# A transformer block on one core: the second attention's output projection and the two normalisations behind it as one block by chunks

## What is computed

```python
x = x + 0.5 * _L0_ffn_ref(_layernorm(x), ...)      # step 1
x = x + _L0_attn_ref(_layernorm(x), ...)           # step 2
x = x + 0.5 * _L0_ffn_ref(_layernorm(x), ...)      # step 3
x = x + 0.5 * _L1_ffn_ref(_layernorm(x), ...)      # step 4, see below
x = x + _L1_attn_ref(_layernorm(x), ...)           # step 5, see below
x = x + 0.5 * _L1_ffn_ref(_layernorm(x), ...)      # step 6, as step 4

def _layernorm(x, eps=1e-05):
    return (x - mean(x)) / sqrt(var(x) + eps)      # over the 128 columns of a row

# the end of _L1_attn_ref: f is the attention's output, 128 wide
    y = f @ Wo.T + bo
    mu, var = mean(y), mean((y - mu) ** 2)
    return x + ln_w * (y - mu) * rsqrt(var + 1e-05) + ln_b    # x is the normalised input of the step

# _L1_ffn_ref: a router picks 2 of 8 experts from its input
    scores = x @ w_gate
    ...
```

## Time and profile before

| | us |
|---|---|
| median of 3 runs (2874.14 to 2876.14) | 2874.9 |
| the profiled execution | 2879.6 |
| its span, first to last instruction | 2877.9 |
| granted TensorE clock over the span, share of full speed | 0.941 |

### The profile page before, as it was taken

One profiled execution on the slowest core, in us unless ns is written; L12 is line 12 of the kernel. 1 busy time (PEld: TensorE's weight loads), 2 busy tenths in 40 slices (PEclk: granted clock), 3 DMA queues, 4 the chain that ended last, 5 costly groups with the idle time before them and its releaser, 6 DMA issues. The chain is left out here.

```text
span 2877.9 us, 60111 instructions
## 1 busy us (share of the span) xinstructions
PE 2457.7 (85%) x18614; PEld 1009.4 (35%) x18614; DVE 2437.3 (85%) x3916; ACT 2254.0 (78%) x2520; POOL 2005.8 (70%) x1255
## 2 busy tenths in 40 slices
PE   4848999997659986999999999999999999983898
PEld 3833333334655662222222222222222222222566
DVE  6778888884676657999999999999999999986765
ACT  4655777776445546899999999999999999992554
POOL 5541222222634656799999999999999999993455
PEclk9978999998678997999999999999999999996799
DMA  4241000000220002000000000000000000000000
GB/s 144 62 128 32 29 28 28 28 28 7 65 63 1 1 1 101 17 18 14 14 15 16 17 14 14 15 14 17 15 14 14 15 16 16 14 1 1 1 12 19
DMA packets 96687, 76.57 MB, mean 27 GB/s; under 512 B 32592, under 2 KB 78168, under 8 KB 96448
## 3 DMA queue, kind: packets, MB, share of 16 engines
q1 hardware_dynamic: 92288, 66.36, 7.9%
q0 software_dynamic: 4288, 8.82, 0.9%
HBM read 47.77 MB, written 24.42 MB: 25 GB/s over the span
## 5 line engine op out<-in xcount | busy, mean ns | idle before, releaser
L1960 POOL TENSOR_TENSOR a_sg<-a_sg,all_f0w 128x1568 f32<-128x1568 f32 x256 | 904.9, 3535 | 21.4
L2103 ACT ACTIVATE a_pt<-a_pb 128x1024 f32<-128x1024 f32 x512 | 698.1, 1363 | 13.6 <-PE a_pb L2010 13.6
L2178 DVE TENSOR_REDUCE a_mx<-a_pm 128x1 f32<-128x1024 f32 x507 | 613.7, 1210 | 13.5 <-PE a_pm L2010 11.9
L2189 DVE TENSOR_SCALAR a_sg<-a_pa 128x1024 int32<-128x1024 int32 x512 | 615.3, 1202 | 8.0 <-PE a_pa L2010 8.0
L2112 ACT ACTIVATE a_sg<-a_sg,a_parh 128x2048 f32<-128x2048 f32 x256 | 599.7, 2343 | 15.3 <-POOL a_sg L1960 15.3
L2028 PE MATMUL a_po<-a_pt,a_Vh 128*32 128x512 f32 x2048 | 541.1, 607 | 64.7 <-ACT a_osb L2122 62.5
L2116 ACT ACTIVATE a_sg<-a_sg 128x2048 f32<-128x2048 f32 x256 | 578.7, 2261 | 0.1
L2028 PE MATMUL a_po<-a_sg,a_Vh 128*32 128x512 f32 x2048 | 541.1, 607 | 0.0
L1957 POOL TENSOR_SCALAR all_f0w<-a_sg,a_parh 128x1568 f32<-128x1568 f32 x256 | 513.8, 2007 | 31.3 <-DVE a_sg L2189 28.6
L1770 ACT ACTIVATE a_pt<-a_ring 128x1024 f32<-128x1024 f32 (+2 forms) x384 | 313.7, 846 | 150.7 <-PE a_ring L1697 147.3
L1842 DVE TENSOR_REDUCE a_mx<-a_ring 128x2 f32<-128x1024 f32 (+3 forms) x384 | 359.1, 955 | 74.3 <-PE a_ring L1680 55.3
(11 more groups left out here) (282 smaller groups left out, 4578.8 us busy)
## 6 DMA issues: line engine op xcount, KB each, us to landing
all_Q<-q_parts SPq DMA_DIRECT2D x256, 48.0 KB
all_K<-k_parts SPq DMA_DIRECT2D x256, 48.0 KB
k_parts<-p_parts SPq DMA_DIRECT2D x16, 384.0 KB, 3.0
e_recs<-routed_rows SPq DMA_DIRECT2D x70, 64.5 KB, 1.8
all_Q<-a_rows SPq DMA_DIRECT2D x256, 2.0 KB
q_parts<-p_parts SPq DMA_DIRECT2D x16, 192.0 KB, 2.4
q_parts<-p_parts SPq DMA_DIRECT2D x8, 384.0 KB, 2.6
a_Vh<-all_V SPq DMA_DIRECT2D x64, 36.0 KB, 1.8
```

What stands on the lines that cost most here:

```text
L1960: nc.gpsimd.tensor_tensor(buf[:, :, 0:CUT], buf[:, :, 0:CUT], sums, ALU.mult)\
L2103: nc.scalar.activation(pt[(j - LT) % 4][:, i, :], pb[:], ACT.Exp, scale=SC)\
L2178: nc.vector.tensor_reduce(mx[:, (j // PER) % 2, t:t + 1], top[:], AX.X, ALU.max)\
L2189: nc.vector.tensor_scalar(sg[(j - ls) % 4][:, i, :].bitcast(I32), pa[:].bitcast(I32), SIGN_OFF, None, ALU.bitwise_and).then_inc(abs_done, 1)
```

## The change

`ln_transposed` is replaced by `norm_split`, and for the second attention `project_out` is drawn into it (argument `front`); `project_out` itself is left with the first attention's case alone. The new block goes by chunks of 4 tiles in steps: in step s, chunk s is turned, chunk s-1 is projected and its statistics and scale are made, chunk s-2 gets its first normalisation, chunk s-3 is added to X and gets its second statistics and scale, chunk s-4 is normalised, chunk s-5 is turned and leaves PSUM, chunk s-6 goes to the router. Without `front` (n4) the same loop begins at s = 2 and holds the later half alone.

Both normalisations move from DVE to ACT (`normalise_y`, `normalise`: one instruction per tile, scale and bias per row, as `norm_project` does). The Newton step gets another form and a last instruction that makes the bias. POOL adds ln_b for all 8 chunks at the block's start, then does one chunk's multiplication by ln_w and one chunk's low part per step. With `front` the turned rows go to the buffer `all_V` in place of `all_XNT`, which still holds the attention's output; without it the incoming rows of n4 are loaded into `all_XNT`.

```diff
-def ln_transposed(nc, tag, X, XNT, ident, split=None, router=None, incoming=None):
+def norm_split(nc, tag, X, XNT, ident, split, router, incoming=None, front=None):
...
+        steps = range(0 if front else 2, NCH + 6)
...
             @block.vector
...
+                def scale(c, var_ready, root_ready, steps_done, root, t, var, inverse, agg, shift, done):
+                    k = tiles(c)
+                    dve.wait_ge(var_ready, c + 1)
+                    dve.wait_ge(root_ready, c + 1)
+                    link = Chain(dve, steps_done, 3 * c)
+                    link(nc.vector.tensor_tensor(t[:, k], root[:, k], root[:, k], ALU.mult))
+                    link(nc.vector.scalar_tensor_tensor(t[:, k], t[:, k], -0.5, var[:, k], ALU.mult, ALU.mult))
+                    link(nc.vector.scalar_tensor_tensor(inverse[:, k], t[:, k], 1.5, root[:, k], ALU.add, ALU.mult))
+                    nc.vector.scalar_tensor_tensor(shift[:, k], agg[:, k, 0], -1.0, inverse[:, k], ALU.mult, ALU.mult)\
+                        .then_inc(done, 1)
...
+                for s in steps:
+                    if front and inside(s - 1):
+                        attended(s - 1)
+                    if inside(s - 3):
+                        rows(s - 3)
+                    if front and inside(s - 1):
+                        scale(s - 1, yve_ready, yrs_ready, ynewton, yrs, yt, yve, yrstd, ymv, yoffset, yscaled)
+                    if inside(s - 3):
+                        scale(s - 3, ve_ready, rs_ready, newton, rs, t1, ve, rstd, mv, offset, scaled)
...
             @block.gpsimd
...
+                if front:
+                    pool.wait_ge(weights_in, loads)
                     for c in range(NCH):
-                        low(c)
+                        nc.gpsimd.tensor_tensor(X[:, tiles(c), :], X[:, tiles(c), :],
+                                                lb[:].unsqueeze(1).broadcast_to([P, 4, D]), ALU.add).then_inc(lb_added, 1)
+                for s in steps:
+                    if front and inside(s - 2):
+                        weigh(s - 2)
+                    if inside(s - 5):
+                        low(s - 5)
...
             @block.scalar
...
+                def normalise(c):
+                    act.wait_ge(scaled, c + 1)
+                    if c >= XR:
+                        act.wait_ge(turned, c - XR + 1)
+                    for q in range(4):
+                        k = 4 * c + q
+                        nc.scalar.activation(xn[:, c % XR, q, :], X[:, k, :], ACT.Identity, bias=offset[:, k:k + 1],
+                                             scale=rstd[:, k:k + 1]).then_inc(xn_ready, 1)
...
+                for s in steps:
+                    if front and inside(s - 2):
+                        normalise_y(s - 2)
+                    if inside(s - 4):
+                        normalise(s - 4)
+                    if front and inside(s):
+                        copy_in(s)
+                    if front and inside(s - 1):
+                        root(s - 1, yve_ready, yve, yrs, yln_var, yrs_ready)
+                    if inside(s - 3):
+                        root(s - 3, ve_ready, ve, rs, ln_var, rs_ready)
+                    if inside(s - 5):
+                        evacuate(s - 5)
...
             @block.tensor
...
+                for s in steps:
+                    if front and inside(s - 1):
+                        project(s - 1)
+                    if front and inside(s):
+                        turn_in(s)
+                    if inside(s - 5):
+                        turn(s - 5)
+                    if inside(s - 6):
+                        route(s - 6)
...
-            lambda: project_out(nc, "o5", X, tiles, ident, a1, a1_in, True),
-            lambda: ffn_second("6", out_v),
+            lambda: ffn_second("6", out_v, front=(tiles, a1, a1_in)),
```

More of the change, by code:

```diff
@@ L97, in ln_transposed @@
         mv = m.sb("mv", [P, NT, 2])
[L98 to L112, removed]
+        ve, rs, t1, rstd, offset = (m.sb(n, [P, NT]) for n in ("ve", "rs", "t1", "rstd", "offset"))
+        xn = m.sb("xn", [P, XR, 4, D])
+        pt = m.ps("pt", [P, 2, CH])
+        psr = m.ps("psr", score.shape)
@@ L119, in _ @@
                 def _(sp):
[L120 to L123, removed]
+                    for c in range(NCH):
+                        sp.dma_start(XNT[:, c * CH:(c + 1) * CH].rearrange("p (k d) -> p k d", d=D),
+                                     incoming[c * CH:(c + 1) * CH, :].rearrange("(k p) d -> p k d", p=P))\
+                            .then_inc(came[c], 16)
@@ new lines, in _ @@
+                if front:
+                    dve.wait_ge(weights_in, loads)
+                for s in steps:
[7 more added lines that the diff above has]
+                        scale(s - 3, ve_ready, rs_ready, newton, rs, t1, ve, rstd, mv, offset, scaled)
@@ L207, in _, with turn_in, project @@
+                act.wait_ge(routed, 1)
+                nc.scalar.activation(score[:], psr[:], ACT.Copy).then_inc(scored, 1)
             @block.tensor
             def _(pe):
+                def turn_in(c):
+                    if c >= 2:
+                        pe.wait_ge(f_copied, c - 1)
+                    for q in range(4):
+                        last = nc.tensor.transpose(ptr[:, c % 2, q * P:(q + 1) * P], F[4 * c + q], ident[:])
+                    last.then_inc(f_turned, 1)
+                def project(c):
+                    pe.wait_ge(f_copied, c + 1)
+                    if c >= 2:
+                        pe.wait_ge(y_in, c - 1)
+                    for q in range(4):
+                        last = nc.tensor.matmul(psy[:, c % 2, q, :], fT[:, c % 2, q * P:(q + 1) * P], woT[:],
+                                                start=True, stop=True)
+                    last.then_inc(y_done, 1)
@@ L210, in route, with turn @@
+                def turn(c):
+                    pe.wait_ge(xn_ready, 4 * c + 4)
+                    if c >= 2:
+                        pe.wait_ge(evacuated, c - 1)
+                    for q in range(4):
+                        last = nc.tensor.transpose(pt[:, c % 2, q * P:(q + 1) * P], xn[:, c % XR, q, :], ident[:])
+                    last.then_inc(turned, 1)
                 def route(c):
@@ L1379, in _ @@
             def _(act):
-                def copy(c):
+                for c in range(NCH):
                     act.wait_ge(turned, c + 1)
@@ L2280, in ffn_first, with ffn_second @@
                           returned, n, *((begin, loaded) if n == 0 else ()))
-        def ffn_second(tag, out=None, incoming=None):
+        def ffn_second(tag, out=None, incoming=None, front=None):
             with ExitStack() as inner:
```

250 lines of the change are left out of this document (89 added, 161 removed).

## The result

The changed kernel takes 2856.9 us (median; 2855.0 to 2857.4), the kernel before 2875.5 beside it: a ratio of 0.9933, interval 0.9916 to 0.9950, or 18.6 us less. The forecast was 2857.3 us and 17.6 us less. The profiled execution took 2857.0 us, with a span of 2855.3.

What follows compares the result with a forecast made beforehand. The bound was taken to be DVE's queue plus a lead-in and lead-out that other engines do not overlap. Joined block -12.8 us (66.9 for 79.7) and n4 -4.8 sum to -17.6, giving 2857.3 us; range 2848 to 2867.

Steps and rivals of the forecast that it cites:

- DVE's work: Joined block: additions, statistics and Newton steps take DVE 5.5 us a chunk, 44.0 us for 8 chunks.
- Lead-in, roots, lead-out: Joined block: 4.1 us to the first bias addition, 2.6 us of root waits in four steps, 6.7 us at the end.
- Waits behind GpSimd: Joined block: DVE instructions held up by POOL, 9.5 us in sum: 2.7 in chunk 0, 5.6 at multiplications, 1.2 at low parts.
- The last term: Last two steps of the joined block: POOL's low part meets DVE's addition to X, 1.2 us (0 to 9).
- the prediction's first reading of rows 6: Old kernel's trace: a DVE instruction of 0.17 us took 2.31 because POOL's multiplication was running, ending at 2640.02.
- n4: Fourth normalisation by chunks: 3.4 us a chunk, lead-out 6.7, low parts 0.5; 37.3 us against 42.1, -4.8 us.
- ACT and PE: Joined block: a step is 6.0 us of work for ACT, and 6.0 us for PE at half clock.
- (b): ACT and DVE go in lockstep; root waits of 0.8 us in some 9 steps lose 7 us: 2864.5; chance 0.2.
- the cover of the roots: Joined block: ACT's roots are ready 0.5 us before DVE wants them; each further delay costs its own length.
- (a): POOL costs DVE nothing, its instructions find the gaps: 57.4 and 36.8 us, time 2847.3 us; chance 0.2.
- (c): The gain is given back by ACT's load and longer waits: block 78 us, n4 unchanged, time 2873; chance 0.06.
- (d): Slower: POOL and DVE always exclude each other, block 85.4 us, n4 46.0, +9.6 us, time 2884.5; chance 0.04.

Runs made afterwards that it cites:

- the extra one: Whole change plus one more GpSimd multiplication of 512 columns in each of 8 steps: joined stretch 67.4 us against 65.4, 18.0 us less than the kernel before.
- the improved version: Whole change with three edits together (ln_b additions early, no variance instruction, rows of X first): joined stretch 57.4 us, 25.4 us less than the kernel before.
- the last run: Whole change with those three edits, and GpSimd instead of ScalarE makes the high parts: joined stretch 59.1 us, 23.0 us less than the kernel before.
- the two halves: Two runs with one half of the change each: n4 only, 5.4 us less than the kernel before; o5 and n6 joined only, 14.1 us less.

## Why the prediction was right, point by point

**DVE's work.** 5.5 us a step was too much by 0.18. Without waits a step takes 5.32 us (2620.41 to 2625.72 in the run with GpSimd's work made small). The statistics had been priced to the end of the variance instruction; where nothing waits for that one, the next starts 0.08 us after it, not 0.17 (2633.47 and 2633.55 above). That is 1.4 us for 8 chunks, and nearly all of the 1.5 us by which the block is shorter than forecast (65.4 against 66.9); two other errors, of about 1 us each, cancel, as the next two paragraphs show.

**Lead-in, roots, lead-out.** First bias addition at 2600.58, 4.0 us behind the first turn (4.1 forecast); four root waits shown as about 0.6 (0.65); from the last Newton instruction's start to the end of the scores 6.85 us (6.7). The third root wait, in step 9, was priced too low: with GpSimd's work made small it is 1.61 us, because ACT's normalising stands ahead of that root. In the whole change 1.0 of it is hidden under the overlong variance instruction.

**Waits behind GpSimd.** 9.5 us forecast, 9.4 found as overlong instructions, 8.4 of them on the path: chunk 0 about 2.5 (2.7), seven variance instructions of y 5.9 together (5.6), one at the end 1.0 (1.2). They came as 1.2 or as 0.6 us long, by the phase, and not as 1.0 each. The last term was wrong in its mechanism, and its size is luck: the low parts at the end come 0.3 us behind the addition to X, so the addition keeps its 0.69 us and GpSimd waits (1.43 us instead of 1.16). What takes 1.18 us there is X's variance instruction, behind the last multiplication, and that cost nothing. That these are waits behind GpSimd is shown by the runs that move or shrink its work (2.5 and 7.6 us back), and that they cost only where the instructions meet, by the extra one. The multiplication that the prediction's first reading of rows 6 rests on, the one that ends at 2640.02, is not among those rows; before the change it was

```profile
2636.75 3.27 POOL L1407 TENSOR_TENSOR o_y<-o_y,all_lw 128x1024 f32<-128x1024 f32 x1 [2.96 <-DVE o_y L1447]
```

**n4.** 37.3 forecast, 36.3 found: a step takes 3.33 us instead of 3.4 (again the end of the statistics), and the 0.5 us allowed for low parts were not needed. There GpSimd waits: its low parts, which come 0.3 us behind VectorE's additions, show 1.42 us instead of 1.15, the additions 0.69.

```profile
842.25 0.69 DVE L177 TENSOR_TENSOR all_X<-all_X,all_XNT 128x512 f32<-128x512 f32 x1
...
845.58 0.68 DVE L177 TENSOR_TENSOR all_X<-all_X,all_XNT 128x512 f32<-128x512 f32 x1
...
848.90 0.69 DVE L177 TENSOR_TENSOR all_X<-all_X,all_XNT 128x512 f32<-128x512 f32 x1
```
```profile
849.18 1.42 POOL L207 TENSOR_TENSOR 4_XL<-all_XNT,4_XH 128x512 f16<-128x512 f32 x1 [21.11 <-ACT all_XNT L256]
```

**ACT and PE.** 6.0 us a step was too much for both. ACT's row of four takes 1.65 us, but the next row begins about 1.55 after its start, and a copy of 0.58 is followed after 0.48; a full step is 5.35 us (the three windows of the improved version). PE is busy for 5.29 at half clock. Since both lay under VectorE's 5.7 to 6.3 us, this did no harm here; but for rival (b) it made the cover of the roots look thinner than it was, and VectorE waits for no root in a full step.

**The rivals.** (a) is wrong by 8.4 us of waits on the path; its own figure, 2847.3 us, lies just outside the range that is said to hold most of it. (b) did not happen in this kernel's full steps, but the three edits together come near it: 5.41 us a step, ACT full, VectorE waiting for roots 0.35 us a step (0.20 and 0.15); the loop through ACT and VectorE is the next limit, as far as the last run shows it. (c): no loss can be seen, by the two halves. (d) is refuted by the extra instruction.

**The total.** The two stretches gave -20.1 us (-14.3 and -5.8) where -17.6 were summed; the medians differ by 18.6 and the two profiled executions by 22.6. The profiled execution of before lay 4.7 us above the median of the runs shown, that of after 0.1 above its own, so a distance carried over as if it were fixed was not. That the median was met to 0.4 us is therefore better than the sum deserves; what held is the working by stretches, to 1.5 and 1.0 us.

## What to carry to other kernels

Where one engine's instructions hold up another's, as GpSimd's did VectorE's here, price the neighbour by where its instruction falls, not by how long it is: 1.26 us of GpSimd under VectorE's statistics cost nothing, the same 1.26 us against an instruction of 0.17 cost up to 1.1, and taking away the instruction that was hit moved the wait to the next one. Joining two stages paid here when the fullest engine gave up work at the same time (10.0 us for both); with the normalising left on it, the joined form was slower than the two blocks. Price steps from start to start, in rows of the same form, and ask of the last instruction of a price whether the next one really waits for it.

## What the runs showed of the hardware

- VectorE's waits behind GpSimd are hidden in durations: an instruction of 128x4 elements took 0.62 to 1.26 us instead of 0.16, and none of that was shown as idle time.
- An instruction with one input in SBUF waits too: the variance TENSOR_SCALAR (0.17 us) took up to 1.23. BATCH_NORM_STATS2 (0.87 for four), its aggregation (0.36 for four) and an addition with one input in PSUM (0.65 to 0.69) never did, beside any GpSimd instruction. "Who interferes with whom", in "SBUF — State Buffer" of the Trainium skill, counts tensor_scalar among the operations that can use both ports, which agrees; it doesn't name the statistics instructions.
- GpSimd loses as well when it comes second: 1.76 us for a multiplication of 1.27.
- PE's granted clock was 0.50, the lower of its two levels, in all of the joined block but two steps, where it was 0.77 on the mean. They follow a step in which PE was busy for 5.28 of 6.32 us; in the second of them PE was busy for 2.28 of 6.32, and behind it the clock was 0.50 again. With the three edits together it was 0.81 in the step of 5.41 us right behind one in which PE had been busy for 5.29 of 5.41.
